# A selective scan beside a graph product: u's gate as one Silu group, and products moved from VectorE to ScalarE and GpSimd

## What is computed

```python
xc, z = split(h @ w_in)
u  = silu(conv4(xc))                       # causal convolution of 4 taps along the nodes
dbc = u @ w_xp                             # 16 + 16 + 16 columns: rank of dt, B, C
dt = softplus(dbc[:, :16] @ w_dt + b_dt)
# for each of 16 states: h_t = exp(dt_t * A) * h_{t-1} + dt_t * B_t * u_t
y  = sum_n(h_t[n] * C_t[n]) + u * D_skip
y  = (y * silu(z)) @ w_out
```

## Time and profile before

| | |
|---|---|
| median of 3 runs | 2455.79 us (2452.02 to 2457.14) |
| the profiled execution | 2455.74 us, its span 2453.8 us |
| mean granted clock of TensorE | 0.959 |
| busy over the span | PE 91%, DVE 77%, ACT 62%, POOL 46% |
| second stage, the scan | about 1143 us to 2218 us |

### The profile page before, as it was taken

The page is one execution under the profiler, slowest core; times in us unless marked ns, Lnnn a source line. Parts: engine busy times, 40 slices in busy tenths (PEclk is TensorE's granted clock), DMA queues, the critical chain, the costliest instruction groups (busy, mean ns, idle before and its releaser), DMA issues.

```text
span 2453.8 us, 26042 instructions
## 1 busy us (share of the span) xinstructions
PE 2233.8 (91%) x8852; PEld 1397.0 (57%) x8852; DVE 1878.5 (77%) x2158; ACT 1527.7 (62%) x2424; POOL 1139.9 (46%) x914
## 2 busy tenths in 40 slices
PE   7998999999999999988999999999999987765998
PEld 4444545454554555546766666666666663433886
DVE  5666778677768775324999998989999998996765
ACT  4667676767676854424665757566666756663444
POOL 2101222222121313303887878888887887891000
PEclk9999999999999999999999999999999998688999
DMA  5232332333332323233323232323323220113121
GB/s 210 95 122 97 101 120 79 120 98 106 97 112 93 105 97 118 86 105 110 114 95 112 87 120 88 116 89 107 117 88 117 87 88 20 50 45 112 35 77 43
DMA packets 116310, 238.06 MB, mean 97 GB/s; under 512 B 8226, under 2 KB 65954, under 8 KB 115794
## 3 DMA queue, kind: packets, MB, share of 16 engines
q1 hardware_dynamic: 107106, 204.00, 25.5%
q0 software_dynamic: 8528, 31.36, 3.6%
q10 hardware_dynamic: 544, 1.05, 0.1%
HBM read 216.06 MB, written 20.32 MB: 96 GB/s over the span
## 4 chain that ended last, share of the span: by engine, by line
PE 47%; DVE 16%; POOL 12%; ACT 12%; issue 12%; DMA 0%; DVEq 0%; ACTq 0%; SPq 0%; POOLq 0%
PE ps L633 13%; POOL dB L2238 8%; DVE h L1419 6%; PE ps L675 3%; DVE acc L1391 2%; PE ps L797 2%; PE ps L771 2%; DVE wgt L1105 2%; ACT wgt L1606 2%; PE ps L919 2%; ACT ps L1606 2%; POOL acc L2221 2%; ACT th L1606 2%; POOL du L2234 2%; PE ps L701 1%
## 5 line engine op out<-in xcount | busy, mean ns | idle before, releaser
L2238 POOL TENSOR_TENSOR dB<-du,bc 128x512 f32<-128x512 f32 x512 | 656.8, 1301 | 90.8 <-DVE h L1419 87.4
L1419 DVE TENSOR_TENSOR_SCAN h<-ps,hst,dB 128x512 f32<-128x512 f32 x512 | 643.9, 1273 | 45.9 <-ACT ps L1606 38.3
L633 PE MATMUL ps<-wgt,msg 128*128 128x512 f32 x1024 | 504.3, 607 | 16.8 <-DVE wgt L1105 15.2
L1606 ACT ACTIVATE ps<-dt,cols 128x512 f32<-128x512 f32 x512 | 351.4, 687 | 268.0 <-DVE h L1419 266.2
L675 PE MATMUL ps<-raw,msg 128*128 128x256 f32 x1792 | 452.8, 389 | 0.9 <-ACT hb L1606 0.9
L919 PE MATMUL ps<-consts,h 128*128 128x128 f32 x2048 | 335.9, 292 | 99.2 <-DVE acc L1391 54.3
L919 PEld LDWEIGHTS ps<-consts,h 128*128 128x128 f32 x2048 | 256.7, 149 | 270.9 <-DVE acc L1391 111.4
L675 PEld LDWEIGHTS ps<-raw,msg 128*128 128x128 f32 x1792 | 331.8, 196 | 74.1 <-issue 39.3
L633 PEld LDWEIGHTS ps<-wgt,msg 128*128 128x128 f32 x1024 | 189.7, 194 | 225.2 <-issue 193.4
L1606 ACT ACTIVATE wgt<-wgt 128x1024 f32<-128x1024 f32 x256 | 258.6, 1047 | 65.9 <-DVE wgt L1098 63.5
L2221 POOL TENSOR_TENSOR acc<-acc,part 128x512 f32<-128x512 f32 x160 | 210.4, 1315 | 82.8 <-ACT part L1606 79.1
(11 more groups left out here) (318 smaller groups left out, 3481.2 us busy)
## 6 DMA issues: line engine op xcount, KB each, us to landing
raw<-in_adjT SPq DMA_DIRECT2D x256, 512.0 KB, 3.6
bc<-tmp_bc SPq DMA_DIRECT2D x64, 512.0 KB, 4.8
E<-tmp_bc POOLq DMA_DIRECT2D x32, 512.0 KB, 4.0
xb<-in_xT POOLq DMA_DIRECT2D x8, 512.0 KB, 4.8
tmp_x<-xb POOLq DMA_DIRECT2D x8, 512.0 KB, 4.8
x<-tmp_x SPq DMA_DIRECT2D x8, 512.0 KB, 5.2
tmp_x<-x SPq DMA_DIRECT2D x8, 512.0 KB, 3.7
raw<-tmp_xn SPq DMA_DIRECT2D x8, 512.0 KB, 4.0
```

The lines of the kernel that those rows point to most:

```text
L633: x = e.matmul(P[d][:, :], msg[:, j, d * 128:(d + 1) * 128], wgt[g % NW][:, l, :], start=j == 0, stop=j == NJ - 1)
L1419: e.tensor_tensor_scan(hr[n % 3][:, m, :], PS[4 + k % 2].t[:, :], dBr[k % 4][:, :], hst[:, n % 16, m:m + 1], ALU.mult, ALU.add).then_inc(S ...
L1606: return e.activation(out, in_, func, bias=bias, scale=scale)
L2238: e.tensor_tensor(dBr[k % 4][:, :], du[:, m, :], bcr[i % 3][:, n % 2, :], ALU.mult).then_inc(S("dB"), 1)
```

## The change

1. `adder`: for n = 0 all of s = 0 to 3 are "scalar" (in the last block s = 1 stays "tensor"). Before only s = 0 was. For s = 1, GpSimd takes n = 2 to 12 (before 4 to 11).
2. u's gate: the taps' weights are not halved any more. After the fourth convolution ScalarE does two Silu of 128x1024 in place, one after the other; the Tanh and VectorE's L1334 are gone. L873 waits for the second Silu.
3. Softplus: ScalarE reads each PSUM bank twice, Relu(x + b) into dt and Abs(x + b) into th1, then Exp and Ln in pieces of 128x512. VectorE adds the two (a plain addition of 128x1024).
4. Ticks: `pre_b` has 71 instead of 73; m = 1 of the convolution takes 8 ticks instead of 10; VectorE's product with the normalization's factor (L1312) comes one tick later.

```diff
 def adder(ib, n, s):
+    if s == 1 and ib == NB - 1:
+        return "tensor"
+    if n == 0:
+        return "scalar"
     if s == 0:
-        return "scalar" if n == 0 else "gpsimd" if n < 14 else "vector"
+        return "gpsimd" if n < 14 else "vector"
     if s == 1:
-        return "tensor" if ib == NB - 1 else "gpsimd" if 4 <= n < 12 else "vector"
+        return "gpsimd" if 2 <= n < 13 else "vector"
     return "vector"
...
-        NP, NPA, NSA, NPB, NPO = 64, 55, 62, 73, 18
+        NP, NPA, NSA, NPB, NPO = 64, 55, 62, 71, 18
...
-            e.tensor_scalar(cols[:, HALVED], cols[:, HALVED], 0.5, None, ALU.mult).then_inc(S("setup"), 1)
...
-                yield from (None, None, None, None, None)
+                yield from [None] * 6
                 v = preb_use(ib, 1)
                 w.wait_ge(S("rr1"), 2 * ib + 2)
                 e.tensor_tensor(hb[:, :, :], hb[:, :, :], two(v.ps), ALU.mult).then_inc(v.evac, 1)
...
-                        what = u[p][:, m - 1:m + 1, :]
-                        w.wait_ge(S("tanh1"), n_th)
-                        e.scalar_tensor_tensor(what, th1[:, :, :], 1.0, what, ALU.add, ALU.mult).then_inc(S("th1r"), 1)
...
-                        e.scalar_tensor_tensor(what, what, 0.0, th1[:, :, :], ALU.max, ALU.add).then_inc(S("th1r"), 1)
+                        e.tensor_tensor(what, what, th1[:, :, :], ALU.add).then_inc(S("th1r"), 1)
...
-                        act(th1[:, :, :], u[p][:, m - 1:m + 1, :], ACT.Tanh).then_inc(S("tanh1"), 1)
...
+                for k in range(2):
+                    for x in (preb_use(ib, 2 + 4 * k), preb_use(ib, 4 + 4 * k)):
+                        w.wait_ge(x.evac, x.n)
+                    what = u[p][:, 2 * k:2 * k + 2, :]
+                    act(what, what, ACT.Silu).then_inc(S("silu1"), 1)
...
+                for q in range(2):
+                    for m in (2 * q, 2 * q + 1):
+                        b, at = preb_use(ib, 11 + m), 12 * ib + 6 * q + m % 2
+                        yield
+                        w.wait_ge(b.full, b.n)
+                        act(dtt[p][:, m, :], b.ps[:, :], ACT.Relu, bias=col("bdt", m)).then_inc(S("relu1"), 1)
+                        yield
+                        w.wait_ge(S("th1r"), 2 * ib + q)
+                        act(th1[:, m % 2, :], b.ps[:, :], ACT.Abs, bias=col("bdt", m)).then_inc(b.evac, 1)
+                    yield
+                    for k in range(2):
+                        b = preb_use(ib, 11 + 2 * q + k)
                         w.wait_ge(b.evac, b.n)
+                        act(th1[:, k, :], th1[:, k, :], ACT.Exp, scale=-1.0).then_inc(S("abs1"), 1)
                         yield
+                    for k in range(2):
+                        w.wait_ge(S("abs1"), 4 * ib + 2 * q + k + 1)
+                        act(th1[:, k, :], th1[:, k, :], ACT.Ln, bias=1.0).then_inc(S("ln1"), 1)
                         yield
+                    yield
```

More of the change, by code:

```diff
@@ L865, in pre_b @@
                     yield from (None, None)
-                    yield from [None] * (4 if m % 2 else 2)
+                    yield from [None] * (4 if m == 3 else 2)
                 yield
                 b = preb_use(ib, 10)
-                w.wait_ge(S("th1r"), 4 * ib + 2)
+                w.wait_ge(S("silu1"), 2 * ib + 2)
                 w.wait_ge(S("d_wxd"), 32)
@@ L1312, in pre_b @@
                 e.tensor_tensor(hb[:, :, :], hb[:, :, :], two(v.ps), ALU.mult).then_inc(v.evac, 1)
-                yield from [None] * 5
-                n_th = 4 * ib
+                yield from [None] * 4
                 for m in range(4):
@@ L1381, in gather @@
                         w.wait_ge(made.evac, made.n)
[L1382 to L1385, removed]
-                        else:
[L1387 to L1391, removed]
+                        if j - 4 in HANDED:
+                            w.wait_ge(S("summed"), HANDED[j - 4] + 1)
+                        else:
+                            w.wait_ge(hT_use(j - 4).evac, hT_use(j - 4).n)
+                        e.scalar_tensor_tensor(acc[:, s, :], b.ps[:, :], c, acc[:, s, :], ALU.mult, ALU.add).then_inc(b.evac, 1)
                 def gates(ib):
@@ L1598, in act @@
             def act(out, in_, func, scale=1.0, bias=0.0, accum=None):
-                need = {ACT.Ln: LNEXP, ACT.Exp: LNEXP, ACT.Tanh: TANH, ACT.Silu: SILU, ACT.Gelu: GELU}.get(func)
-                if func == ACT.Exp and table[0] == TANH:
-                    need = TANH
+                need = {ACT.Ln: LNEXP, ACT.Exp: LNEXP, ACT.Silu: SILU, ACT.Gelu: GELU}.get(func)
                 if need is not None and table[0] != need:
@@ L1880, in pre_b @@
                 w.wait_ge(S("du"), 4 * (ib - 1))
-                for m in range(4):
-                    b = preb_use(ib, 11 + m)
-                    yield
-                    w.wait_ge(b.full, b.n)
-                    act(dtt[p][:, m, :], b.ps[:, :], ACT.Identity, bias=col("bdt", m)).then_inc(b.evac, 1)
-                    yield
-                    if m % 2:
-                        at = 4 * ib + 2 * (m // 2)
-                        w.wait_ge(b.evac, b.n)
-                        w.wait_ge(preb_use(ib, 10 + m).evac, preb_use(ib, 10 + m).n)
-                        w.wait_ge(S("th1r"), n_th)
-                        act(th1[:, :, :], dtt[p][:, m - 1:m + 1, :], ACT.Abs).then_inc(S("abs1"), 1)
-                        yield
-                        w.wait_ge(S("abs1"), at + 1)
-                        act(th1[:, :, :], th1[:, :, :], ACT.Exp, scale=-1.0).then_inc(S("abs1"), 1)
-                        yield
-                        w.wait_ge(S("abs1"), at + 2)
-                        act(th1[:, :, :], th1[:, :, :], ACT.Ln, bias=1.0).then_inc(S("tanh1"), 1)
-                        n_th += 1
-                        yield from (None, None, None, None)
+                for q in range(2):
[7 more added lines that the diff above has]
+                        act(th1[:, m % 2, :], b.ps[:, :], ACT.Abs, bias=col("bdt", m)).then_inc(b.evac, 1)
+                    yield
+                    for k in range(2):
+                        b = preb_use(ib, 11 + 2 * q + k)
+                        w.wait_ge(b.evac, b.n)
+                        act(th1[:, k, :], th1[:, k, :], ACT.Exp, scale=-1.0).then_inc(S("abs1"), 1)
[4 more added lines that the diff above has]
+                        yield
+                    yield
                 b = preb_use(ib, 15)
```

34 lines of the change are left out of this document (12 added, 22 removed).

## The result

The changed kernel takes 2411.52 us (median of 4 runs, 2410.33 to 2412.75); the kernel before, run beside it on the same chip, takes 2455.22 us (2452.02 to 2457.14). The ratio is 0.9823, 95% interval 0.9806 to 0.9840: 44 us off where I forecast 29. The span of the profiled execution went from 2453.8 to 2410.7 us, a difference of 43.1, at a mean granted clock of 0.967 (before 0.959).

What follows compares the result with a forecast made beforehand. DVE and PE were taken as near full together, each limiting different stretches; 0.4 + 2.0 + 2.0 = 4.4 us per block, times seven about 31 us, 29 taken off 2455.7 gave 2427 us, range 2402 to 2453 (8 in 10).

Steps and rivals of the forecast that it cites:

- DVE's work and waits off: Per block, 6.1 us of DVE's work and 6.7 us of its waits go; DVE busy near 122 us.
- the hole: New wait of DVE's scan for exp 49 behind u's two Silu on ACT: 2.9 us per block, bounds 1.0 and 4.7.
- L873 covered by 1.1 us: PE's w_xp product waits for the second Silu, which other PE work was to hide by about 1.1 us.
- signs of being wrong: Wait near step 49 over 6 us, L873 waiting for ScalarE, late GpSimd `du`, or n = 0 copies waiting for transposes.
- From the gates to 1600.3: PE's gapless stretch behind the gates: of 3.2 us of DVE sums off, only about 0.4 us gets through.
- From there to L873: From PE's gapless end to the w_xp product: PE's gaps, at most 1.8 us plus 0.4; 2.0 us taken.
- From L873 to the gates: ACT's 20 us against 23, less the tail of DVE's new wait: 2.0 us saved per block, bounds 0 and 3.5.
- serial chain ahead of the first scan: Before the first scan, two Silu and a load against one Tanh and L1334 were to cost 1 us.
- small mismatches: Allowance for mismatches of the fixed order: of about 31 us saved over the kernel, 29 us were forecast.
- Rival 1: DVE alone is the bound: 9 us per block, 2393 us; milder form 6 us per block, 2413; chance 0.14.
- Rival 2: PE is the bound throughout: under 0.7 us per block, no measurable change, 2451 to 2460 us; chance 0.10.
- Rival 3: u's two Silu at exp 49 make DVE and PE wait; at a 9 us wait 12 us slower, 2468; chance 0.13.

Runs made afterwards that it cites:

- a_relief: The changed kernel with a quarter of the second stage's graph product left out on PE: 2388.00 us, ratio 0.9719.
- b_relief: The kernel before with a quarter of the second stage's graph product left out on PE: 2446.62 us, ratio 0.9955.
- a_load2: The changed kernel with one more load of the same table between u's two Silu: 2425.97 us, ratio 0.9875.
- a_grid73: The changed kernel on the old grid: 73 ticks, m = 1 with its two ticks, L1312 one tick earlier: 2441.97 us, ratio 0.9941.
- b_silu: The kernel before with only the Silu group, the taps' weights, the 71 ticks and L1312's tick; old adder and softplus: 2433.38 us, ratio 0.9910.
- b_adder: The kernel before with only the new `adder`: 2445.05 us, ratio 0.9955.
- a_hole: The changed kernel with GpSimd's sums of n = 10, s = 0 and 1, given back to VectorE: 2412.16 us, ratio 0.9823.
- a_wxp: The changed kernel with both halves of the product with w_xp issued together behind the second Silu: 2411.83 us, ratio 0.9824.
- b_soft: The kernel before with only the new softplus: 2446.49 us, ratio 0.9960.
- a_all: The changed kernel with w_xp's product in one piece, later relu copies of the graph product's half, and n = 10 back on VectorE: 2409.17 us, ratio 0.9810.

## Why the prediction was right in direction and short in size

- **What bounds the kernel.** Two engines near full, each limiting a different stretch: right. The three parts alone give their own savings in three different stretches, and a_relief against b_relief shows that PE was not what set L1308 to L873 before and is now.
- **DVE's work and waits off, the hole.** Right: DVE busy 122.8, L1312's and Tanh's waits gone, taps from 2.5 to 1.3 (1.2 off, 1.8 forecast), hole 3.3 for 2.9. Beside it the scan's other waits for ACT are 2.4 us (5.7 - 3.3).
- **L873 covered by 1.1 us.** Size off: it waits 0.17 us, so one of the signs of being wrong did come, if weakly. PE arrives earlier than I had it, as the saving before it was larger; a_load2 shows no cover left. Of the other signs, PE is again without a gap for over 33 us behind the gates.
- **"From the gates to 1600.3: ... only about 0.4 us gets through."** Right: 0.3 by the same cut. The 3.2 us of DVE's sums were held by PE, as forecast.
- **"From there to L873: PE's gaps, at most 1.8 us plus the 0.4; I take 2.0 in all."** This is the step that failed, measured 5.7 in the block compared: 1.7 ahead of L1308 and 4.0 behind it. Ahead of L1308 it is 0.3 of a shorter wait and 1.4 of PE at the lower clock, which the timeline of before had in full view (1.91 us for L567) and which I took for fixed work; that part exists in three of the five blocks only. Behind L1308 the gaps closed by 1.4 as worked out. The bound "at most" was wrong, because it took PE's work between two events as given, while the grid of 71 ticks changes which of the graph product and the transposes stand before L873: 2.6 us less. a_grid73 puts the 2.6 us back (49.69 busy, of 52.94) and adds a gap of 2.07, and b_silu alone has the same 47.32. I had worked out step positions for every moved tick of DVE and ACT and not counted PE's records between them.
- **"From L873 to the gates: ... 2.0."** As a whole too large by 1.6: dbc to `du` gave 1.9, near the 2.0 forecast from ACT's 20 us (0.3 in block 4, where the clock fell), but the product with w_xp was cut in two and lost 1.5. Its two ticks lie at steps 49.49 and 50.00 now, so step 49.5's transposes fall between them; before they lay at 49.83 and 50.33, in one step. That was one more division like the ones I made.
- **Sum.** 2.0 + 4.0 - 1.5 + 1.9 = 6.4 us in the block compared, and 6.0 on average over the seven, for 4.4. The least is 3.3 us in block 4, the most 9.0 in block 6 (143.08 to 134.10). The serial chain ahead of the first scan showed no loss: its preparation takes 61.3 us for 61.6 where I had 1 us more. The 2 us that I took off the sum for small mismatches went the wrong way and stood on no row.
- **Rival 1**, DVE alone: its mild form's 2413 is near the result for another reason. b_adder brought through 1.4 us for 3.8 us taken off DVE, and a_hole added DVE work at no net cost. What I gave for this rival was misread: 1914.98 to 2054.82 is the last third of block 5 and the first two thirds of block 6, and not a block without a graph product. Block 6 from `du` to `du` is 143.08 us before.
- **Rival 2**, PE throughout: false for the kernel before (b_relief), nearer the truth for the changed one.
- **Rival 3**, the Silu group turns the sign: it didn't, but by its ticks. On the old grid PE waits 2.07 us at this place, and by addition the group alone would be 3 to 7 us of loss. I had it as depending on when ACT ends the group; what decides is which part copies and transposes are queued around it.
- **Open**: why the granted clock falls in one block and not in the next, and so why edits that shorten L873 to dbc meet a stretch of lower clock behind it in every block (a_wxp, a_hole). The blocks show its price there, 1.6 to 1.7 us; what makes it fall was not separated.

## What to carry to other kernels

When a change moves instructions in a fixed order, count for every engine what then stands before and after the event that the next stage hangs on, not only the gaps: work moved behind such an event is a saving even where the engine has no gap at all. A mean or a gap says nothing of a matmul at the lower clock, so read the durations of equal rows side by side (1.91 and 1.02 us) before taking an engine's busy time as work. And price an added block of work by its neighbours in the queue: with the same Silu group the stretch up to L873 was 4.0 us shorter than before on one grid and 1.6 us longer on another, where the group lies a third of a step later.

## What the chip showed that I had not expected

- TensorE's granted clock changes what a stretch of a few us costs without any change in the work: eight records of the graph product took 1.89 or 3.46 us, a product of the normalization 1.02 or 1.91. Where another engine waited for it, one such stretch cost 1.2 to 1.7 us of a block of 133; in b_adder, where none did, it cost nothing.
- No wait of PE alone explains it. In the kernel before, the clock fell behind a wait of 1.92 to 1.97 us in blocks 2, 3 and 5 and held behind one of 1.98 in block 1; in b_soft it held behind 1.87 to 1.98 in all blocks; and in block 2 of a_hole PE's rows show no wait in the 10 us ahead of the fall.
- That stretch moves: a saving of 1.0 to 1.2 us per block ahead of dbc was lost whole in a_wxp and a_hole, so that three different orders have the same time within 0.1%, and in a_all it moved from behind dt to ahead of L1308.
- A table load in the middle of a group costs its 1.29 us and nothing more on ScalarE, but 1.7 us of the block's period, where it stands on the path: 1.4 by the wait, the rest by the clock.
